# A GNN, mixer and expert layer on one core: an engine no-op ahead of each of 880 gathers

## The reference

```python
xn = _layernorm(x, axis=-1)
# GNN, once forward and once backward (source and destination exchanged):
proj = jnp.einsum('ni,rio->rno', feat, W)          # 16 projections of all nodes
m = proj[etypes, src_idx] + bias                   # one row of 256 for each edge
m = m * norm_per_edge[:, None]
return segment_sum(m, dst_idx, num_segments=n)     # sum by destination node
# then
x = x + gnn(xn) + mix(xn)                          # linear attention and an MLP
x = x + ffn(_layernorm(x))                         # 8 experts, the best 2 of each token
```

## Time and profile before

| | us |
|---|---|
| median of 3 runs | 2248.73 |
| lowest and highest run | 2247.24, 2249.34 |
| the profiled execution's own time | 2245.63 |
| its span, first to last instruction | 2243.7 |
| PE busy | 2015.8 (90%) |
| DVE busy | 1138.3 (51%) |
| POOL busy | 1027.6 (46%) |
| ACT busy | 605.0 (27%) |

### The profile page before, as it was taken

How to read it: one execution, slowest core, us unless ns; L and a number is a source line. 1 busy time by engine, 2 the same in 40 slices (tenths; PEclk the granted TensorE clock), 3 DMA queues, 4 the chain that set the end, 5 groups by cost and what they waited for, 6 DMA issues and landing times.

```text
span 2243.7 us, 26429 instructions
## 1 busy us (share of the span) xinstructions
PE 2015.8 (90%) x8235; PEld 1379.3 (61%) x8235; DVE 1138.3 (51%) x2452; ACT 605.0 (27%) x1262; POOL 1027.6 (46%) x1014
## 2 busy tenths in 40 slices
PE   7999999889999999898878788898989669999997
PEld 3456544355555555454545555677777668888897
DVE  4999950256666564433566656544455841111121
ACT  2333333211221221111422221222222552222242
POOL 0000000366666666666566666666665113333332
PEclk9999999999999999999899999999999579999999
DMA  7432335455555555556644444332334384444473
GB/s 276 158 136 95 134 155 229 159 158 177 179 178 179 178 168 182 178 181 165 184 144 138 146 138 122 90 90 87 87 90 80 128 288 112 125 116 120 128 194 67
DMA packets 136486, 333.20 MB, mean 149 GB/s; under 512 B 25344, under 2 KB 65952, under 8 KB 135072
## 3 DMA queue, kind: packets, MB, share of 16 engines
q1 hardware_dynamic: 80064, 199.64, 24.5%
q0 software_dynamic: 52992, 130.09, 23.1%
q10 hardware_dynamic: 3296, 1.80, 0.3%
HBM read 202.71 MB, written 128.71 MB: 148 GB/s over the span
## 4 chain that ended last, share of the span: by engine, by line
PE 80%; issue 6%; another core or an unknown queue 5%; DVE 4%; ACT 3%; DMA 2%; DVEq 0%; POOL 0%; SPq 0%; ACTq 0%; POOLq 0%
PE bank L679 29%; PE bank L748 15%; PE bank L1947 9%; PE bank L1958 8%; PE bank L1867 4%; PE bank L1876 4%; PE bank L586 3%; DVE arena L773 1%; PE bank L1777 1%; PE bank L1805 1%; DMA table_fwd<-arena 1%; PE bank L1765 1%; PE bank L1844 1%; PE bank L1916 1%
## 5 line engine op out<-in xcount | busy, mean ns | idle before, releaser
L679 PE MATMUL bank<-arena,work 128*128 128x512 f32 x1600 | 741.9, 600 | 14.2 <-ACT arena L672 9.0
L773 DVE TENSOR_TENSOR arena<-arena,bank 128x257 f32 x880 | 370.8, 421 | 529.7 <-PE bank L748 284.1
L748 PE MATMUL bank<-arena 128*128 128x257 f32 x1760 | 499.2, 396 | 71.1 <-DVE arena L773 37.6
L725 POOL DMA_INDIRECT arena<-table_bwd,arena x440 | 428.3, 974 | 237.4 <-issue 99.0
L725 POOL DMA_INDIRECT arena<-table_fwd,arena x440 | 437.2, 994 | 212.8 <-issue 99.8
L679 PEld LDWEIGHTS bank<-arena,work 128*128 128x128 f32 x1600 | 301.3, 192 | 296.5 <-issue 270.8
L672 ACT ACTIVATE arena<-bank 128x512 f32<-128x512 f32 x400 | 238.5, 598 | 777.4 <-PE bank L679 551.7
L748 PEld LDWEIGHTS bank<-arena 128*128 128x128 f32 x1760 | 327.7, 197 | 194.8 <-issue 153.7
L1017 POOL DMA_INDIRECT out<-xn,work x56 | 89.4, 1597 | 250.9 <-DVE xn L192 181.3
L1947 PE MATMUL bank<-xn,arena 128*128 128x256 f32 (+1 forms) x1120 | 203.0, 340 | 0.0
L734 DVE TENSOR_TENSOR arena<-cst,arena 128x512 f32<-128x512 f32 x220 | 151.2, 689 | 102.0 <-PE bank L679 102.0
(11 more groups left out here) (315 smaller groups left out, 1563.8 us busy)
## 6 DMA issues: line engine op xcount, KB each, us to landing
table_fwd<-arena SPq DMA_DIRECT2D x100, 512.0 KB
table_bwd<-arena SPq DMA_DIRECT2D x100, 512.0 KB
arena<-in_W SPq DMA_DIRECT2D x35, 1024.0 KB
arena<-in_W SPq DMA_DIRECT2D x2, 4096.0 KB, 14.3
arena<-table_fwd,arena POOLq DMA_INDIRECT x440
arena<-table_bwd,arena POOLq DMA_INDIRECT x440
work<-x_transposed SPq DMA_DIRECT2D x50, 128.0 KB
mix_rows<-arena SPq DMA_DIRECT2D x25, 256.0 KB
```

The costliest lines, as they stand in the source:

```text
L679: last = pe.matmul(ps[4 + s % 2][:, :], xT[t % 2][:, k * P:(k + 1) * P], ar(W_off[d] + k * 4096 + c * 512, 512), start=(k == 0), stop=(k = ...
L725: e.indirect_dma_start(msg[b][:, 0:C], None, table[d], bass.IndirectOffsetOnAxis(ap=idx[d][:, n % TE:n % TE + 1], axis=0)).then_inc(s_ga[b ...
L748: pe.matmul(ps[sum_bank(n)][:, 0:W], oh[b], msg[b], start=True, stop=True).then_inc(s_sm, 1)
L773: vec.tensor_tensor(to, to, ps[sum_bank(n)][:, 0:W], ALU.add).then_inc(s_ac, 1)
```

## The change

In `gather`, `e` is GpSimd's engine. One instruction that does nothing is put ahead of each gather's wait. It is not put ahead of the experts' indirect transfers.

```diff
         def gather(e, n):
 
             d, b = n // TE, n % RING
+            e.engine_nop()
             G.wait(s_sm, n - RING + 1)
             e.indirect_dma_start(msg[b][:, 0:C], None, table[d], bass.IndirectOffsetOnAxis(
                 ap=idx[d][:, n % TE:n % TE + 1], axis=0)).then_inc(s_ga[b], 16)
```

## The result

The changed kernel took 2258.70 us (median of 5 runs, 2253.29 to 2259.24) against 2248.73 us before (5 runs, 2245.89 to 2252.18). The ratio is 1.0035, with a 95% interval of 1.002 to 1.005. So it is slower, by some 8 to 10 us. The profiled execution took 2259.24 us, its span is 2257.5 us, 13.8 us over that of before. It is the slowest of the five, and the profiled execution of before (2245.63 us) was faster than any of its five, so the two traces differ by some 4 us more than the medians.

The account below looks back on a forecast made before the run. The prediction took the order and number of PE's products as the bound; no-ops hide in POOL's waits except 0.4 us at the start, so 2248.73 + 0.4 = 2249.1 us, with a range of 2244 to 2262 us.

Parts of the forecast that it names:

- a no-op that costs POOL just over 0.204 us: Between gathers: a no-op of 0.204 to 0.235 us makes POOL the bound, up to 14 us, at most 2262 us; 2%.
- PE's order is the bound, and POOL's room decides: Gather stretches: PE waits only if a no-op costs POOL over 0.204 us forward or 0.251 us backward.
- the lead: Gathers ahead of their sums: at least 13.2 us can be lost once in each direction, 0.030 us for each gather.
- The threshold of 0.204 us: Forward gathers: 0.174 us waiting for a buffer plus 0.030 us of lead; beyond it, 0.01 us costs 4.4 us a direction.
- A no-op costs POOL 0.10 us, between 0.03 and 0.13 us: Between two gathers: the no-op's assumed cost, taken from POOL's smallest memsets; 88 us of POOL time for 880.
- the cover: Forward gathers: 0.174 us each of waiting for a buffer hides the no-ops; without it they cost 88 us in all.
- 0.4 us at the start: First four gathers, ring empty: each no-op delays a sum, 4 x 0.10 us on the path, between 0.1 and 0.5 us.
- Fetching 880 more instructions: Instruction queues: 3.3% more to fetch, 1.0 us if PE's 30.1 us of unexplained waiting grew in proportion; only in the range.
- fetching stalls: Instruction queues: 4 or 5 more packets each stop all engines for 6.0 us, 27 us more, 2276 us; 2%.
- if the distances are as said and the time still moves: Sign of error in the trace after: then the transfers' spacing or fetching matters, and PE's or DVE's idle time shows where.
- The starts that were to stay within 1 us: First and last gather starts of each direction: to stay near 420.7, 1065.4, 1074.6 and 1731.1 us.
- The idle time ended by sums: POOL's waits for a free buffer: should shrink as no-ops use them up; 76.7 us forward and 97.4 us backward before.

Follow-up runs that it names:

- e4: The same 880 no-ops at the start of GpSimd's list, none by the gathers, against the kernel before: 2232.74 us, ratio 1.0006.
- e1: Two no-ops ahead of each gather instead of one, 1760 in all, against the kernel before: 2242.22 us against 2231.03 us, ratio 1.0043.
- e9: No no-op, a second, already implied wait at 864 gathers, against the kernel before on a slower chip: 2254.80 us against 2249.08 us, ratio 1.0025.
- e10: Eight no-ops in a row ahead of each eighth gather, against the kernel before on a slower chip: 2252.47 us, ratio 1.0017.
- e2: Four no-ops ahead of each gather, 3520 in all, against the kernel before: 2248.12 us, ratio 1.0069.
- e6: 880 no-ops in DVE's list, none in GpSimd's, against the kernel before on a faster chip: 2080.31 us, ratio 1.0001.
- e12: 880 no-ops in DVE's list, none in GpSimd's, once more on another faster chip, against the kernel before: 2082.53 us, ratio 1.0003.
- e8: The changed kernel itself, one no-op ahead of each gather, against the kernel before on a faster chip: 2079.48 us, ratio 0.9999.
- e3: A sequencer no-op in place of the engine's, left out at build, so equal to the kernel before: 2230.50 us, ratio 0.9994.
- e7: Sixteen no-ops ahead of each gather, against the kernel before on a faster chip: 2299.41 us against 2080.17 us, ratio 1.1061.

## Why the prediction was right or wrong

**The range held, the forecast's side did not.** 2258.7 us lies in 2244 to 2262 us, but the time moved by more than 0.2%, for which the prediction had 15%, while 80% stood on no change. That the time lies in the range is luck as far as the mechanism goes. The room up to 2262 us was made for fetching, at 1.0 us, and for a no-op that costs POOL just over 0.204 us. The second did not happen, and no run shows what the time was spent on.

- *PE's order is the bound, and POOL's room decides.* Right for the chip of the first measurement: PE's busy time is the same and no sum waits for a gather in the steady part. On the other kind of chip some sums do wait (16.6 us, 26 times). There sixteen no-ops cost what the room says, 217 us without the lead, against 219 us measured. The threshold of 0.204 us itself belongs to a chip on which PE stands; on the other kind the room is 0.02 us for each gather, so that there a no-op that took the 0.10 us I assumed would have cost about 880 x (0.10 - 0.023) = 68 us, an estimate.
- *A no-op costs POOL 0.10 us, between 0.03 and 0.13 us.* Too high at either end. Gathers stayed 1.25 us apart instead of the forecast 1.28 to 1.38; four no-ops added 0.02 us, and the slope from there is 0.021 us each. One or two disappear in the 0.30 us. The step that failed was to take the gathers' distance of 0.30 us for a sign that nothing overlaps there. What I named as the cover, the 0.174 us of waiting for PE, was not even used.
- *0.4 us at the start.* Not there, for the same reason: the fourth gather starts 3.98 us behind the first, as before.
- *Fetching 880 more instructions, left out of the sum and put at 1.0 us at most in proportion.* The sum had no other place for a cost of an added instruction than POOL's pace and this one, and 8 to 10 us were measured. This is the term that was mis-sized, if the cost is in it. The extra time arises beside the gathers (e4 against e1), it comes with a plain wait as well (e9), and it goes with the packets fetched in that stretch: 7 more cost 6 to 10 us (the change, e9), or 4 us (e10), 14 cost 10 us (e1), 28 cost 15 us (e2). The packets only count the instructions, so this fits any cost for each instruction as well. The rival "fetching stalls" had 4 or 5 packets where 7 came, and 27 us at a chance of 2%; if the cost is fetching, neither the size nor the chance was right.
- *What would show it wrong*: "if the distances are as said and the time still moves". That is the case that came, with distances even shorter than said. The starts that were to stay within 1 us moved: the last forward one by 4.0 us, the first and last backward ones by 5.7 and 12.8 us. The idle time ended by sums, which was to shrink, stayed at 159.7 us.

**What stays open.** Shown: instructions added to GpSimd's list cost something beside the gathers and nothing measurable ahead of them, the cost is not GpSimd's pace, and it was seen on the chips where PE stands anyway and not on the two others. Not shown: that it takes GpSimd's list (e6 and e12 met chips of the other kind), why PE stands, and whether an added instruction acts by being fetched, by being issued or by being recorded in the trace, since all of these go together in every kernel that ran. In the trace of the changed kernel 14 of PE's 53 idle times over 1.2 us between 430 and 1750 us had an 8 KB packet of the queue q14 start in the 6 us before them, where chance would give 12; that speaks against the simplest form, in which each fetch stops PE.

The recording deserves more suspicion than the experiments gave it. On the slower chips a part of the trace is missing. These are the forward gathers in the list of transfers, for the changed kernel on the chip of the first measurement and on that of e8; the last number is the median time to landing, and the first trace has none for them:

```profile
arena<-table_fwd,arena POOLq DMA_INDIRECT x440
...
arena<-table_fwd,arena POOLq DMA_INDIRECT x440, 3.2
```

The first trace holds 15185 updates of semaphores, the second 30053, from the same program. Up to 400 us they are alike (3683 and 3702); from 400 to 1750 us it is 7257 against 23221. The other traces go the same way: 14948 to 15738 updates on every slower chip, 30049 to 30074 on the two faster ones. So updates are lost on the chips on which PE stands, and next to none of those before the gathers. A wait put down to "remote" can be one whose update was lost: the counts of "remote" are not counts of stands. The joint restart of three engines does not depend on that. Nor does it hide late gathers, since the transfers' own packets are all there. By them a gather's last packet ends 2.6 us (median) behind the gather's start on both chips. In the changed kernel's first trace 99% of the sums start more than 10 us behind that, half of them more than 17 us, while on the chip of e8 a quarter start within 2 us of it. That PE stands because records can't be taken away fast enough, and that each added instruction costs by its own record there, is a rival that no run speaks against: the no-ops of e4 lie before 314 us, where no updates are missing. It is not shown: every execution on record has a span and a clock from the profiler, so there is no time without recording to compare with.

The intervals of e9 and e10 both begin just above zero, so that their sizes should not be leaned on.

## What to carry to other kernels

To price an added instruction on an engine that is not the bound, first find the distance between its neighbours in an unbroken run: if something fixed stands there, the instruction may vanish in it, and what counts is the room left over for each round, which was eight to nine times smaller on another chip. An effect of a few tenths of a per cent should be measured on more than one chip before it is explained, and a run that adds instructions should be checked by the number of instructions on its page: e3 had none of its own. Where a wait has no releaser, see first whether the trace has all its semaphore updates.

## What the runs showed of the hardware

- One program took 2249, 2231, 2249, 2080 and 2081 us in five measurements. The difference lies in the two stretches with gathers, 1340 against 1160 us. PE is idle there for 177.9 against 50.5 us, in stands such as the one of 3 us shown above, and the clock is granted less fully (0.94 against 0.98 over the second stretch). What sets the chips apart is not known.
- On the slower chips half of the semaphore updates are missing from the traces, 15185 against 30053 for the changed kernel. Up to 400 us, before the gathers, the counts hardly differ (3683 and 3702).
- A no-op of GpSimd's engine behind an indirect DMA adds 0.021 us to the distance between gathers from about the third on: with one, two, four, eight and sixteen the idle time before the gather is 0.30, 0.30, 0.32, 0.40 and 0.57 us. In the trace of e7 the records of the sixteen start 0.021 us apart, the first as the gather ends and the last 0.26 us ahead of the next gather. The Trainium skill, GPSIMD Engine Reference, section "Instruction dispatch", has tens of cycles for an instruction's dispatch; 0.021 us is at the low end of what that makes at the page's 1.2 GHz, an estimate of 0.02 to 0.08 us.
- The 0.30 us between gathers can hold one or two no-ops at no cost. That agrees with the Trainium skill, Perfetto Trace Analysis, section "DMA Instruction — SWDGE (GPSIMD)", by which the profile has only such a DMA's end and no start mark: the idle time ahead of it need not be idle.
